# Self attention of a decoder layer: how the softmax weights are transposed and exponentiated

## What is computed

```python
R_hat = (1.0 + jnp.exp(vv)) / (1.0 + jnp.exp(vv - wv * R))
scores = jax.nn.relu(jnp.einsum('bhqd,bhkd->bhqk', q, k)) * R_hat[None]
scores = jnp.where(causal[None, None], -jnp.inf, scores)
attn = jax.nn.softmax(scores / np.sqrt(hd).astype(x.dtype), axis=-1)
ctx = jnp.einsum('bhqk,bhkd->bhqd', attn, val)
...
x = _layernorm(x + _L0_attn_ref(x, ...), axis=-1)
x = _layernorm(x + _L0_xattn_ref(x, ctx_1024, ctx_1024, ...), axis=-1)
x = _layernorm(x + _L0_ffn_ref(x, ...), axis=-1)
```

## Time and profile before

| | us |
|---|---|
| median of 3 runs (lowest to highest) | 2508.53 (2507.49 to 2508.64) |
| profiled execution, its own time | 2508.33 |
| span of the profile | 2506.5 |
| PE busy over the span | 2432.2 (97%) |
| DVE busy | 1535.0 (61%) |
| ACT busy | 1251.4 (50%) |
| POOL busy | 1319.6 (53%) |

### The profile page before, as it was taken

One profiled execution on the slowest core, in us unless ns is written; L12 is line 12 of the kernel. 1 busy time (PEld: TensorE's weight loads), 2 busy tenths in 40 slices (PEclk: granted clock), 3 DMA queues, 4 the chain that ended last, 5 costly groups with the idle time before them and its releaser, 6 DMA issues.

```text
span 2506.5 us, 58637 instructions
## 1 busy us (share of the span) xinstructions
PE 2432.2 (97%) x22240; PEld 2089.1 (83%) x22240; DVE 1535.0 (61%) x2593; ACT 1251.4 (50%) x2455; POOL 1319.6 (53%) x1058
## 2 busy tenths in 40 slices
PE   7999988998999999999999999999999899999999
PEld 7888866887888888888888888888888698998998
DVE  7555567963667766666766666676666725345342
ACT  3544453104666666666666666666666652322311
POOL 4766554313656666566666656666665533333322
PEclk9999998998999999999999999999999999999999
DMA  7554455633776777777767777777776861011010
GB/s 225 162 149 137 136 159 186 242 136 101 194 190 187 188 185 187 189 192 190 190 184 186 187 188 194 189 186 186 188 187 178 234 184 64 30 34 54 8 38 22
DMA packets 259626, 391.61 MB, mean 156 GB/s; under 512 B 123165, under 2 KB 140573, under 8 KB 259357
## 3 DMA queue, kind: packets, MB, share of 16 engines
q1 hardware_dynamic: 234780, 337.66, 46.9%
q10 hardware_dynamic: 24576, 50.36, 8.4%
HBM read 134.11 MB, written 52.43 MB: 74 GB/s over the span
## 4 chain that ended last, share of the span: by engine, by line
PE 72%; DVE 1%; issue 1%; DMA 1%; SPq 1%; ACT 1%; POOL 0%; ACTq 0%; DVEq 0%; POOLq 0%
PE D_ps_p L68 41%; PE D_ps_s L1725 7%; PE D_ps_p L1751 6%; PE E_ps_u L68 5%; PE E_ps_g L68 5%; PE E_ps_d L68 5%; PE E_ps_y L68 3%; SPq L1175 1%; ACT D_e L1398 0%; DVE D_neg_max L1534 0%; PE E_ps_t L1778 0%; DMA D_pT<-D_turned 0%; DMA E_w_int<-in_w_gate 0%; DVE D_turned L1548 0%; DMA D_values<-in_ctxT 0%
## 5 line engine op out<-in xcount | busy, mean ns | idle before, releaser
L1282 POOL TENSOR_SCALAR D_e<-D_e,D_inv 128x722 f32<-128x722 f32 x256 | 538.2, 2102 | 540.6 <-DVE D_inv L1540 540.6
L1398 ACT ACTIVATE D_e<-D_ps_s,D_neg_max 128x723 f32<-128x723 f32 x512 | 437.9, 861 | 407.6 <-DVE D_neg_max L1534 358.5
L1534 DVE TENSOR_REDUCE D_neg_max<-D_ps_s 128x1 f32<-128x723 f32 x512 | 439.6, 899 | 314.0 <-PE D_ps_s L1725 314.0
L1548 DVE STREAM_TRANSPOSE D_turned<-D_e 128x768 f32<-128x768 f32 x512 | 496.1, 972 | 6.1 <-DMA D_pT<-D_turned 4.8
L68 PE MATMUL D_ps_p<-D_ctx_high,cross_wk_high 128*128 128x362 f32 (+1 forms) x1024 | 351.0, 343 | 12.9 <-DVE D_ctx_low L1565 12.7
L68 PE MATMUL D_ps_p<-D_ctx_low,cross_wk_high 128*128 128x362 f32 (+1 forms) x1024 | 337.3, 329 | 0.0
L68 PE MATMUL D_ps_p<-D_ctx_high,cross_wk_low 128*128 128x362 f32 (+1 forms) x1024 | 335.9, 328 | 0.0
L68 PE MATMUL D_ps_p<-cross_wv_high,D_ctx_high 128*128 128x512 f32 (+1 forms) x768 | 303.9, 396 | 0.0
L68 PE MATMUL D_ps_p<-cross_wv_high,D_ctx_low 128*128 128x512 f32 (+1 forms) x768 | 303.3, 395 | 0.0
L68 PE MATMUL D_ps_p<-cross_wv_low,D_ctx_high 128*128 128x512 f32 (+1 forms) x768 | 301.7, 393 | 0.0
L1405 ACT ACTIVATE D_e<-D_e,D_inv 128x722 f32<-128x722 f32 x256 | 230.9, 902 | 7.4 <-DVE D_inv L1540 7.4
(11 more groups left out here) (194 smaller groups left out, 5085.5 us busy)
## 6 DMA issues: line engine op xcount, KB each, us to landing
D_pT<-D_turned SPq DMA_DIRECT2D x1536, 96.0 KB, 2.6
D_pT<-D_turned ACTq DMA_DIRECT2D x512, 96.0 KB, 2.6
D_craw<-in_ctxT SPq DMA_DIRECT2D x126, 361.0 KB, 3.7
self_q<-A_q_out SPq DMA_DIRECT2D x10, 640.0 KB, 3.7
self_k<-A_k_out SPq DMA_DIRECT2D x10, 640.0 KB, 3.2
self_v<-A_v_out SPq DMA_DIRECT2D x25, 256.0 KB, 2.1
A_q<-self_q SPq DMA_DIRECT2D x32, 200.0 KB, 3.9
A_k<-self_k SPq DMA_DIRECT2D x32, 200.0 KB, 4.6
```

Source lines behind the costliest of these rows:

```text
L1282: pool.tensor_scalar(head, head, inv[:, 2 * (s % 2):2 * (s % 2) + 1], None, ALU.mult)\
L1398: act.activation(e[n // 2 % 2][:, n % 2, 0:PARTS * PART].rearrange("p (a c) -> p a c", a=PARTS), parts_of(n), ACT.Exp, bias=neg_max[:, n % ...
L1534: dve.tensor_reduce(neg_max[:, n % 4:n % 4 + 1], parts_of(n), AX.XY, ALU.max, negate=True)\
L1548: dve.transpose(turned[quad % 2][:, :, 2 * (s % 2) + h, :].rearrange("p j (t r) -> p t j r", r=32), e[s % 2][:, h, :].rearrange("p (t j r) ...
```

## The change

**Transposing.** The transposes on PE and ACT's copies after them are gone. `e` is now 128 x 16 x 128, cleared once by POOL, and the scaled scores are written straight into it. DVE transposes each 32 x 32 block of `e` in place of the whole (`turn_blocks`, two instructions of 128 x 1024) into `turned`. A block that lies off the diagonal then belongs to other partitions: six DMAs on SP's queue (`move`) carry those of the lower triangle to `pT`; the upper triangle is zero in the weights (causal) and stays cleared. POOL copies the four diagonal blocks (`copy_diagonal`). There is one `turned` and one `pT`.

**Softmax.** POOL's subtraction is gone: ACT takes the exponential head by head, 16 of 100 x 100, with the maximum as bias and the sum as a by-product (`accum_out`), so DVE's sums are gone too. The maximum is taken in two halves of 8 heads.

**Sums.** All 16 matmuls of `weighted_sum` stand together, one step later than before, and are 128 columns wide. `scores` comes after the second unit of a step (it was after the third). The freed bank `ps_t` becomes a third bank for units. The last `weighted_sum` stands behind `project_o(0, 2)`.

```diff
+        e = [sb(f"e{i}", [P, H, P]) for i in range(2)]
+        turned = sb("turned", [P, BLOCKS, H, 32])
+        pT = sb("pT", [P, BLOCKS, H, 32])
...
+        ps_u = [*ps_a, ps_t]
...
+                def move(b):
+
+                    sp.wait_ge(turn_done, 2 * (b + 1))
+                    wait(sp, pv_done, b)
+                    if b == 0:
+                        sp.wait_ge(cleared, 3)
+                    for d in range(1, BLOCKS):
+                        for a in range(d, BLOCKS):
+                            j = a - d
+                            sp.dma_start(pT[32 * j:32 * (j + 1), a, :, :],
+                                         turned[32 * a:32 * (a + 1), j, :, :]).then_inc(moved, 16)
...
+                    if 2 <= s < B + 2:
+                        move(s - 2)
+                    if s >= 4:
+                        store_o(s - 4)
...
+                def copy_diagonal(b):
+                    pool.wait_ge(turn_done, 2 * (b + 1))
+                    wait(pool, pv_done, b)
+
+                    pool.wait_ge(norm_done, 2 * min(b + 2, B))
+                    for a in range(BLOCKS):
+                        rows = slice(32 * a, 32 * (a + 1))
+                        pool.tensor_copy(pT[rows, a, :, :], turned[rows, a, :, :]).then_inc(diag_done, 1)
+                    pool.wait_ge(diag_done, BLOCKS * (b + 1))
...
                 def exps(b, half):
-                    act.wait_ge(sub_done, 2 * b + half + 1)
-                    wait(act, t_done, QUADS * (b - 1))
-                    part = slice(HH * half, HH * (half + 1))
-                    act.activation(e[b % 2][:, part, :], s_rel[b % 2][:, part, :], ACT.Exp).then_inc(exp_done, 1)
-
...
+                    act.wait_ge(max_done, 2 * b + half + 1)
+                    wait(act, inv_done, 2 * (b - 1) + half + 1)
+                    for i in range(HH):
+                        h = HH * half + i
+                        head = e[b % 2][0:T, h, 0:T]
+                        act.activation(head, head, ACT.Exp, bias=neg_max[:, b % 2, h:h + 1],
+                                       accum_out=rowsum[:, half, i:i + 1]).then_inc(exp_done, 1)
...
+                def turn_blocks(b, half):
+                    dve.wait_ge(norm_done, 2 * b + half + 1)
+                    wait(dve, moved, 16 * MOVES * b)
+                    wait(dve, diag_done, BLOCKS * b)
+                    dve.transpose(turned[:, :, HH * half:HH * (half + 1), :].rearrange("p j h r -> p h j r"),
+                                  e[b % 2][:, HH * half:HH * (half + 1), :].rearrange("p h (j r) -> p h j r", r=32))\
+                       .then_inc(turn_done, 1)
...
+                    if c < B:
+                        scale(c)
+                    for half in range(2):
+                        if c < B:
+                            maximum(c, half)
+                        if b >= 0:
+                            turn_blocks(b, half)
+                    if c < B:
+                        invert_sums(c, 0)
+                        invert_sums(c, 1)
...
+                def weighted_sum(b):
+                    pe.wait_ge(v_loaded[b % 3], 16 * (b // 3 + 1))
+                    wait(pe, o_done, b)
+                    pe.wait_ge(moved, 16 * MOVES * (b + 1))
+                    pe.wait_ge(diag_done, BLOCKS * (b + 1))
...
+                        if i == 0 and s >= 3:
+                            weighted_sum(s - 3)
+                        if i == 1 and s < B:
+                            scores(s)
+                project_o(0, 2)
+                weighted_sum(B - 1)
```

More of the change, by code:

```diff
@@ L363, in _ @@
                 stored = 0
-                for s in range(B + 2):
+                for s in range(B + 3):
                     while stored < units_before(s):
@@ L455, in _ @@
                     split_x(1, k)
+                for tile in e:
+                    pool.memset(tile[:, :, :], 0.0).then_inc(cleared, 1)
+                pool.memset(pT[:, :, :, :], 0.0).then_inc(cleared, 1)
                 pool.wait_ge(rhat_step, 2 * QUADS + 1)
@@ L458, in _ @@
                                    base=0, pattern=[[0, H], [-1, T]], channel_multiplier=1).then_inc(rhat_done, 1)
-                for s in range(1, B + 1):
-                    b = s - 1
-                    subtract_max(b, 0)
-                    subtract_max(b, 1)
+                pool.wait_ge(cleared, 3)
+                for s in range(1, B + 2):
+                    if s <= B:
+                        normalise(s - 1, 0)
+                        normalise(s - 1, 1)
+                    if s >= 2:
+                        copy_diagonal(s - 2)
                     for g in range(2, NG):
@@ L642, in scale_max, with maximum @@
+                def maximum(b, half):
+                    heads = slice(HH * half, HH * (half + 1))
                     dve.wait_ge(rel_done, b + 1)
-                    wait(dve, sub_done, 2 * (b - 1))
-                    dve.tensor_reduce(neg_max[:, b % 2, :], s_rel[b % 2][:, :, :], AX.X, ALU.max, negate=True)\
+                    wait(dve, exp_done, H * (b - 2) + HH * (half + 1))
+                    dve.tensor_reduce(neg_max[:, b % 2, heads], e[b % 2][0:T, heads, 0:T], AX.X, ALU.max, negate=True)\
@@ new lines, in invert_sums @@
+                    wait(dve, norm_done, 2 * (b - 1) + half + 1)
+                    dve.reciprocal(inv[:, half, :], rowsum[:, half, :]).then_inc(inv_done, 1)
+                def turn_blocks(b, half):
[5 more added lines that the diff above has]
+                       .then_inc(turn_done, 1)
@@ L793, in scores @@
                     last.then_inc(s_done, 1)
-                def transposes(b, bank):
-                    pe.wait_ge(norm_done, 2 * b + bank // 2 + 1)
-                    wait(pe, pT_done, QUADS * b + bank)
-                    for m in range(4):
-                        last = pe.transpose(ps_t[0:T, m * T:(m + 1) * T], e[b % 2][:, 4 * bank + m, :], ident[0:T, 0:T])
-                    last.then_inc(t_done, 1)
-                def weighted_sum(b, bank):
-                    if bank == 0:
-                        pe.wait_ge(v_loaded[b % 3], 16 * (b // 3 + 1))
-                        wait(pe, o_done, b)
-                    pe.wait_ge(pT_done, QUADS * b + bank + 1)
-                    for m in range(4):
-                        c = (4 * m + bank) * HD
-                        last = pe.matmul(ps_o[HD * m:HD * (m + 1), bank * T:(bank + 1) * T], vs[b % 3][:, c:c + HD],
-                                         pT[bank % 2][:, m, :], start=True, stop=True, tile_position=(0, HD * m))
+                def weighted_sum(b):
[3 more added lines that the diff above has]
+                    pe.wait_ge(diag_done, BLOCKS * (b + 1))
+                    for bank in range(QUADS):
+                        for m in range(4):
+                            c = (4 * m + bank) * HD
+                            last = pe.matmul(ps_o[HD * m:HD * (m + 1), bank * P:(bank + 1) * P], vs[b % 3][:, c:c + HD],
+                                             pT[0:T, :, 4 * bank + m, :], start=True, stop=True, tile_position=(0, HD * m))
                     last.then_inc(pv_done, 1)
```

105 lines of the change are left out of this document (34 added, 71 removed).

## The result

| | before | changed |
|---|---|---|
| median of the runs (lowest to highest), us | 2508.01 (2506.95 to 2508.64) | 2523.22 (2520.86 to 2525.35) |
| profiled execution; its span, us | 2508.33; 2506.5 | 2524.59; 2522.7 |
| PE, DVE, ACT, POOL busy, us | 2432, 1535, 1251, 1320 | 2396, 1548, 1326, 1313 |

The changed kernel is slower: the ratio is 1.0061, 95% interval 1.0043 to 1.0078. That is 15 us more, where 16 less was forecast. The time lies outside the range of 2480 to 2511. PE does 36 us less work, as the change intends, and the gain is lost in waits.

The account below looks back on a forecast made before the run. PE was taken to bound the kernel while units last, then a DVE and POOL loop of 9.4 us. 24.7 - 0.8 - 5.2 - 2.5 = 16.2 gained, so 2492 us; 8-in-10 range 2480 to 2511.

Parts of the forecast that it names:

- PE: PE's work per step: loses 1.4 us, to 8.3 in short steps and 9.37 on average; sums cost 1.36 per round.
- DVE and POOL together: Loop from one second product through copies, transposes, maximum, inversion and first product to the next: 9.4 us, the new pace.
- The 27 steps: Self attention's scaling steps, each the greater of 9.4 and old length less 1.4: 266 against 290.7 us, gain 24.7.
- the rival to which I gave 0.16 and 9 us: Loads of q and k come too late behind moves and stores on SP, so PE waits: 2501; chance 0.16.
- the large loads: Three loads of x and the next stage's loads in front of some moves in the queue: 2.5 us lost in all.
- The four copies overlap: Rival: POOL's diagonal copies on different partitions take 1.0 us instead of 2.44; total 2484; chance 0.22.
- Late moves: Rival: moves land 4.0 us after issue, not 2.6, making their loop 10.6; total 2516, slower than before; chance 0.11.
- Dearer instructions: Rival: an exponential costs 0.45 or a POOL copy 1.0; loops of 10.9 to 11, total 2517 to 2520; chance 0.07.
- The three steps after them: Three steps after the units end: 9.4 + 9.4 + 12.3 = 31.1 us against 30.3, a loss of 0.8.
- The clearing "at no cost": Clearing of `e` and `pT` falls into POOL's wait before the loop: no cost, or some 5 us without that cover.
- The end: Last two transposes and last sums delay DVE's norm work: between 4.4 and 6.4 us, taken as 5.2, passed on in full.

Follow-up runs that it names:

- x2: Changed kernel with POOL copying the previous batch's diagonal blocks between its two products instead of after them: 2512.3 us, ratio 1.0012 to 1.0032.
- x1: Changed kernel with SP issuing the q and k loads once their tile is stored, before the previous step's last units: 2522.6 us, ratio 1.0046 to 1.0079.
- z1: x3 plus clearing at the start of POOL's work, next stage's large loads behind k(31), last weighted sum before the third output projection: 2490.3 us.
- x3: Changed kernel with the edits of x1 and x2 together: 2505.3 us, ratio to before 0.9981 to 1.0000.

## Why the prediction was wrong

**PE.** Right: PE lost its role as bound and waits. Over the 27 steps it is busy for 246.8 us instead of 284.8, 1.41 less per step against 1.4 forecast. The agreement is in part luck: a round of sums takes 1.01 (157.83 to 158.84) where I took 1.36, and part of PE's work runs at the lower clock, 0.96.

**DVE and POOL together, 9.4: the loop that was followed was not the longest.** Most prices held: transpose 1.24 forecast and measured, maximum 0.97 for 0.99, product 1.53 for 1.5, copies 2.61 for 2.44. But I closed the loop over the second transpose, the inversion and the first product (2.94 us). The loop that decides leaves DVE after the second maximum and passes over ACT: eight exponentials and an inversion, then the second product. By the forecast's own prices it is 9.0, with handovers 9.25, which looks harmless. Measured it is longer by 0.25 for eight exponentials (0.36 each instead of 0.33), by 0.17 for the copies, and by 0.2 for two handovers, 0.16 from POOL's product to its copies and 0.13 from the copies to DVE, instead of 0.04 each: 9.9 to 10.0. The loop that I followed, from the second product at 153.08 to the end of the next first product (160.94 and 1.53 more), is 9.39 in the same step, the forecast's 9.4: its size was right, and another loop was longer. I had looked at ACT's loop and POOL's loop each for itself, and not at the one that crosses both. x2, which takes the copies out of it, proves the place: short steps of 9.2.

**The 27 steps.** With 9.9 in place of 9.4, the rule "the greater of that and the old length less 1.4" gives 276.3 (97.8, of which one step rises from 9.6 to 9.9, and 18 x 9.9). Measured were 285.6. Of the other 9.3, part is k and q behind stores and moves in SP's queue, the rival to which I gave 0.16 and 9 us: 4.1 shows in x1, 7.8 once the copies are out of the way. What the rest is was not separated. With both repaired the 27 steps are 267.3 (z1) to 269.9 (x3), against a forecast of 266 plus 2.5 for the large loads. With their short steps of 9.2 the rule gives 263.9, with the large loads 266.4. So as a sum the rule held within 1 to 4 us, but not step by step: in z1 the step from start 8 is 14.6 where it says 9.3, and that from start 7 is 10.0 where it says 11.6. The failed assumption is that an instruction's place in a queue costs nothing beside the bound.

**The four copies overlap** (a chance of 0.22): refuted. The four copies of 32 partitions take 2.61, 0.65 apart. The Trainium skill, page "GPSIMD Engine Reference", section "Instruction dispatch", by which each core starts its next instruction when its own share is done, is not borne out here: the copies lie on different partitions and follow one another all the same.

**Late moves** (0.11): not so in general. The group of issues reads:

```profile
A_pT<-A_turned SPq DMA_DIRECT2D x168, 64.0 KB, 2.0
```

2.0 from issue to landing, the lower bound of the forecast, where I took 2.6; only three waits, 7.6 us. After the repairs they are waited for more often (DVE 16 times, 20.5 us in z1); that they are the bound there no run shows. **Dearer instructions** (0.07): an exponential of 0.36 lies between forecast and bound; the rival's loops of 10.9 to 11 did not come.

**The three steps after them, forecast 31.1, measured 38.7.** The forecast gave the large loads 2.5 in all and no place. In SP's queue they stand in front of k(30):

```profile
354.03 0.37 SPq L328 DMA_DIRECT2D C_oraw<-self_o  x1
...
356.37 0.61 SPq L302 DMA_DIRECT2D A_q<-self_q  x1
357.02 2.21 SPq L302 DMA_DIRECT2D A_k<-self_k  x1
```

They stood there before too, but then k(30) was issued at 349.98, 3.3 ahead of start 29; now it is issued 5.2 behind it, since the six moves (from 349.18, 3.86 us of issues) and a store of the result go in front. I had named the queue and costed only the moves' own loop. Without the large loads in front (z1) it is 31.45, the forecast's figure.

**The clearing "at no cost": 3.1.** It fell beside DVE's making of the table.

```profile
33.04 3.55 POOL L480 MEMSET A_e<- 128x2048 f32 x2
36.53 1.92 POOL L481 MEMSET A_pT<- 128x2048 f32 x1
```

```profile
34.39 4.18 DVE L652 TENSOR_SCALAR A_rhat<-A_rhat,A_ev 100x100 f32<-100x100 f32 x4
...
41.57 0.82 DVE L652 TENSOR_SCALAR A_rhat<-A_rhat,A_ev 100x100 f32<-100x100 f32 x4
```

The series of four takes 4.18 beside the clearing, and the same series in the kernel before 0.82:

```profile
34.67 0.82 DVE L633 TENSOR_SCALAR A_rhat<-A_rhat,A_ev 100x100 f32<-100x100 f32 x4
```

It ends at 38.57, the clearing at 38.45. The series before that one took 3.42 and 3.43 in the two kernels, beside POOL's splitting of tiles. I asked whether POOL had time, and not what POOL's work does to DVE's. So the first scaling was late by 3.1; and the first step is 0.4 longer, by the longer series on ACT, where I had written that it loses nothing else. The Trainium skill, page "SBUF — State Buffer", section "Who interferes with whom", has such a rule: DVE in some of its modes and GpSimd share a port pair, and the second to come waits for the whole instruction of the first. The trace agrees, as far as the ends of the two go; in which mode DVE's operations ran, no view shows.

**The end, 5.2.** From start 31 to the first add it is 25.0 instead of 19.85, 5.2 as forecast. The second add is 6.5 later, since DVE waited 5.37 for `high_o` (4.01 before), which on ACT stood behind the result of the last sum. I had put `high_o` some 5 later, and the end still at 5.2.

**The sum.** Forecast, in us gained: 24.7 (27 steps) - 0.8 (three steps) - 5.2 (end) - 2.5 (large loads) = 16.2. Measured: 5.1 - 8.3 - 6.5 - 3.5 = -13.2, where the last term is the start (3.1 and 0.4) and the large loads are in the first two. The largest miss is the first term, 19.6 of 29.4 us; with it as forecast the other three would have left the kernel 6 us faster than before.

## What to carry to other kernels

When work moves between engines, follow every loop that crosses them, also the one over the engine that has time to spare; a loop 2% below the bound by estimated prices may be the bound. Then write down each queue as it will stand, and ask of each wait what lies behind it: one order on POOL and one on SP were worth 18 us (x3), more than the 15 that the change cost. Two such faults hide one another, so a repair that brings nothing alone (x1) may be half of one that does.

## What the runs showed of the hardware

- Short exponentials are dominated by a fixed part: with a read of the sum they start 0.361 us apart for 100 elements and 0.85 apart for 722, from which I estimate 0.28 that does not depend on the length. 800 elements in one instruction without the read took 0.87. Sixteen short ones take 5.8 us where two long ones took 1.7.
- Four copies of 512 elements on four different groups of 32 partitions take 2.61 us on POOL, 0.65 each, one after another.
- Four short TENSOR_SCALAR operations of DVE took 4.18 us beside POOL's clearing of tiles, 3.42 beside its splitting of tiles, and 0.82 with POOL idle.
- A move of 64 KB between partitions lands 2.0 us after its issue, and the issues are 0.6 apart, so that six of them cost SP 3.7 us, more than the landing.
